# The mask that spreads queries over edges in a graph attention kernel, made by ScalarE instead of VectorE

## The chip, the core and the metric

The kernel runs on one core of a Trainium2 chip. The core has five engines that run side by side and meet only at semaphores: TensorE (PE in the rows) multiplies matrices, VectorE (DVE) and ScalarE (ACT) compute elementwise, GpSimd (POOL) here issues indirect gathers, and SyncE (SP) here watches transfers and loads rows. ACTq, DVEq, POOLq and SPq are the instruction queues (sequencers) of those engines: register work, semaphore waits, loads of registers and DMA issues run there. The metric is the device time of one execution in microseconds (us). The kernel before takes 7133.87 us, the median of 3 runs (7126.53 to 7137.48).

## The reference

Two graph networks run one after the other on 6,250 nodes and 100,000 edges, each with a residual and a layer norm around it. The first is four graph convolutions, which this change does not touch. The second is two attention layers:

```python
xn = _layernorm(x, ln1_g[l], ln1_b[l])
...
q = (xp @ Wq[l] + bq[l]).reshape(n, H, HD)          # k, v likewise
att = jnp.einsum('ehd,ehd->eh', q[dst], k[src]) / scale
att = jnp.nan_to_num(jnp.clip(att, -50.0, 50.0), nan=0.0, posinf=50.0, neginf=-50.0)
m = jax.ops.segment_max(att, dst, num_segments=n)
ex = jnp.exp(att - m[dst])
s = jax.ops.segment_sum(ex, dst, num_segments=n)
alpha = ex / (s[dst] + 1e-16)
msg = (v[src] * alpha[:, :, None]).reshape(-1, D)
aggr = jax.ops.segment_sum(msg, dst, num_segments=n)
x = x + (aggr @ Wo[l] + bo[l])
h = jax.nn.gelu(_layernorm(x, ln2_g[l], ln2_b[l]) @ W1[l] + b1[l], approximate=False)
x = x + (h @ W2[l] + b2[l])
```

Here D = 128, H = 8 heads and HD = 16; `dst` is sorted and falls with a square law on the low node numbers, so the first tiles of nodes have many edges and the last ones few.

## The kernel before, in words

Nodes lie in 49 tiles of 128 (the partitions). Edges are sorted by destination and lie in 196 groups of 4 x 128 = 512 edges, an edge on a partition. A tile's edges are a range of groups `first..last`; the last group of a tile is the first of the next one, since a group can hold edges of both. Six passes run one after the other: p = 0 to 3 are convolutions, p = 4 and 5 the attention layers ("first" and "second" attention pass here). In an attention pass a step of the loop handles one pair of tiles (even, then odd), and beside its edges the node work of earlier pairs in a pipeline: norms, feed-forward product with Gelu, and in the first pass also queries, keys and values of the next layer.

For a group `g` of tile `t` the engines do this:

- GpSimd issues 4 indirect gathers (L1391) of the key and value rows into a ring of 7 groups. It may refill a slot when `groups_freed` says that ScalarE has seen the group's message.
- SyncE loads the group's destination numbers as a row on all partitions, `dst_row` (a ring of 4), waits for the gathers of group `g`, and then says `group_landed` for `g` and `dst_ready` for `g + 1`.
- The node mask `mask_t[node, edge] = (dst_row[edge] == node_id[node])` is 128x512. VectorE makes it (L796). In the profile its tile is called `conv_only`, of which it is a part. It has two slots: slot 0 for the group's own tile and slot 1 for the next tile, used at the last group of a tile, which belongs to both.
- TensorE spreads the queries over the edges: `spread_q` (L1777) multiplies the mask with the tile's query rows, 4 times (8 times at a group of two tiles), and writes `q_ps`. It waits for `mask_t_ready`.
- VectorE multiplies queries with keys (L990), sums per head (L993), clips (L997, L998) and adds (L1001, `logits`). Then it makes the other mask, `masks[edge, node]` for the sums (L808), which waits until TensorE has added the group before.
- ScalarE takes the exp (L1502), VectorE multiplies it with the values into the message (L1005), and TensorE adds it into the tile's sums (`add_group`, L1787). In between TensorE runs 5 filler products (L1758).

The order is written out by hand in `attend_step` of each engine. `weigh` is the VectorE part of a group and stands in front with the mask of group `g + 1` (`ahead`), so a mask is made one group early. `close` ends a tile: the mask of the next tile at the shared last group, some node work, and the mask of the sums. ScalarE's part of a group is only the exp and the word `groups_freed`; between groups it does the node work: column copies with scale and bias (L1518, L1616), the Gelu of a pair (L1629) with a table load before it and one behind it (L1633, with a dummy exp `warm`), the copies of queries, keys and values (L1540, L1541) and the stores. At each step every engine loads the group ranges of its two tiles into registers (L459).

## Time and profile before

| | |
|---|---|
| median of the timed runs | 7133.87 us |
| the profiled execution's own time | 7115.46 us |
| its span | 7112.9 us |
| TensorE busy | 4951.4 us (70%) |
| VectorE busy | 3873.3 us (54%), 10619 instructions |
| ScalarE busy | 678.4 us (10%), 1598 instructions |
| GpSimd busy | 3368.2 us (47%) |
| attention passes | from about 4090 us to the end |

Busy time is the time in which an engine computes; waits, register work and DMA issues are not in it. No engine is busy all the time, so shares do not say what bounds the kernel: for that one reads, stretch by stretch, which wait ends last. In a row of the timeline the bracket is the engine's idle time before the instruction and what ended it. Rows of one line that follow each other are merged (x8, for instance, for the four f32 products of a group).

### The profile page before, as it was taken

How to read it: one execution, taken by the hardware profiler on the slowest of the kernel's cores; microseconds unless marked ns; L12 is line 12 of the kernel's file. 1: busy time of each engine (PE TensorE's matmuls, PEld its weight loads, DVE VectorE, ACT ScalarE, POOL GpSimd, SP SyncE). 2: the span in 40 equal slices, each digit the busy share in tenths (PEclk: the TensorE clock that was granted, in tenths of full speed). 3: DMA queues.
4: the chain of work that ended last, by engine and by line, in shares of the span. 5: the costliest groups of instructions: out<-in, count | busy, mean ns of one | idle time of the engine just before them, and what ended most of it. 6: DMA issues, size and time to landing. Idle time of an engine off the chain costs nothing.

```text
span 7112.9 us, 114495 instructions
## 1 busy us (share of the span) xinstructions
PE 4951.4 (70%) x25317; PEld 3761.7 (53%) x25540; DVE 3873.3 (54%) x10619; ACT 678.4 (10%) x1598; POOL 3368.2 (47%) x3512
## 2 busy tenths in 40 slices
PE   2677656767778778887477666677777666666666
PEld 1121345555666656676455544566666444555555
DVE  8644346663344423444345556677667556666665
ACT  0011100000000000000001100011112100111111
POOL 0000265664555465553666566666443366665441
PEclk9975667668989989999688788899889788888887
DMA  1011323223333333343233244444333244443331
GB/s 47 18 54 72 116 74 91 83 81 104 116 116 120 105 115 112 110 128 104 61 116 98 77 120 120 123 121 121 104 100 87 80 121 118 123 120 104 92 90 49
DMA packets 308014, 695.45 MB, mean 98 GB/s; under 512 B 68843, under 2 KB 118116, under 8 KB 306526
## 3 DMA queue, kind: packets, MB, share of 16 engines
q0 software_dynamic: 146944, 381.90, 19.1%
q10 hardware_dynamic: 94612, 196.31, 8.2%
q1 hardware_dynamic: 66250, 114.82, 5.4%
q8 instruction: 88, 1.44, 0.1%
q14 instruction: 120, 0.98, 0.0%
HBM read 624.93 MB, written 67.83 MB: 97 GB/s over the span
## 4 chain that ended last, share of the span: by engine, by line
PE 32%; DVE 18%; issue 16%; DMA 14%; POOL 10%; DVEq 7%; ACT 2%; POOLq 0%; SPq 0%; ACTq 0%
DMA ring<-rows,idx_stage 12%; POOL ring L1391 10%; PE acc_ps L1853 7%; PE acc_ps L1835 7%; PE q_ps L1777 4%; PE acc_ps L1787 3%; PE bank L1889 2%; DVE wide L990 1%; DVE dots L993 1%; DVE even_rows L582 1%; DVE masks L808 1%; PE bank L2028 1%; PE acc_ps L1747 1%; DVEq L459 1%; DVEq L466 1%
## 5 line engine op out<-in xcount | busy, mean ns | idle before, releaser
L1391 POOL DMA_INDIRECT ring<-rows,idx_stage x3360 | 3329.0, 991 | 2482.3 <-DMA ring<-rows,idx_stage 914.5
L1853 PE MATMUL acc_ps<-ring,masks 128*128 x4800 | 1147.8, 400 | 681.9 <-SPq L1304 352.2
L1853 PEld LDWEIGHTS acc_ps<-ring,masks 128*128 128x128 f32 x4800 | 921.4, 241 | 879.7 <-issue 802.8
L1777 PE MATMUL q_ps<-odd_rows,conv_only 128*128 (+1 forms) x3904 | 733.5, 354 | 710.9 <-DVE conv_only L796 708.4
L788 DVE SCALAR_TENSOR_TENSOR masks<-dst_f,neg_first,lane 128x256 f32<-128x256 f32 x1200 | 546.1, 483 | 1057.7 <-PE acc_ps L1853 891.6
L1777 PEld LDWEIGHTS q_ps<-odd_rows,conv_only 128*128 128x128 f32 x3904 | 648.6, 255 | 782.0 <-issue 778.2
L1787 PE MATMUL acc_ps<-msg,masks 128*128 x3904 | 625.5, 309 | 191.2 <-DVE msg L1005 191.1
L1787 PEld LDWEIGHTS acc_ps<-msg,masks 128*128 128x128 f32 x3904 | 571.8, 216 | 318.3 <-issue 309.9
L1376 POOL COPY idx_stage<-src_idx 128x28 int32 (+1 forms) x126 | 33.1, 262 | 1157.0 <-DVE bias_part L727 809.5
L808 DVE SCALAR_TENSOR_TENSOR masks<-dst_f,neg_first,lane 128x512 f32<-128x512 f32 x488 | 366.6, 751 | 238.7 <-PE acc_ps L1787 231.0
L796 DVE TENSOR_SCALAR conv_only<-conv_only,node_id 128x512 f32 x488 | 243.6, 499 | 438.0 <-SPq L1333 267.3
L1758 PE MATMUL q_ps<-bias_rows,zeros_bf 128*128 128x512 bf16 x1228 | 370.6, 430 | 22.3 <-issue 13.9
L710 DVE TENSOR_SCALAR ring<-ring 128x784 f16 x434 | 184.0, 424 | 316.6 <-PE q_ps L1748 117.8
L1005 DVE TENSOR_TENSOR msg<-ring,msg x392 | 270.8, 691 | 72.0 <-ACT msg L1502 70.9
L889 DVE TENSOR_SCALAR rows<-acc_ps,dinv 128x256 f32<-128x256 f32 (+1 forms) x147 | 64.0, 435 | 398.0 <-PE q_ps L1762 333.2
L993 DVE TENSOR_REDUCE dots<-wide 128x32 f32<-128x512 f32 x392 | 269.0, 686 | 13.4
L990 DVE TENSOR_TENSOR wide<-q_ps,ring 128x512 f32 x392 | 270.2, 689 | 7.3 <-PE q_ps L1777 2.0
L582 DVE TENSOR_TENSOR even_rows<-lane_bf,even_rows 128x1024 bf16<-128x1024 bf16 x196 | 238.6, 1217 | 52.9 <-PE bank L1713 43.1
L1502 ACT ACTIVATE msg<-logits 128x32 f32 x392 | 89.1, 227 | 1681.5 <-DVE logits L1001 1681.5
L1758 PEld LDWEIGHTS q_ps<-bias_rows,zeros_bf 128*128 128x128 bf16 x1450 | 160.1, 110 | 142.0 <-issue 57.7
L1713 PE MATMUL bank<-even_rows 128*128 128x49 bf16 x1568 | 90.9, 210 | 186.5 <-DVE even_rows L584 186.5
L1661 ACT ACTIVATE wide<-q_ps 128x512 f32<-128x512 f32 (+2 forms) x75 | 38.9, 519 | 1899.7 <-PE q_ps L1762 1899.7
(278 smaller groups left out, 6202.0 us busy)
## 6 DMA issues: line engine op xcount, KB each, us to landing
conv_only<-dst_rows SPq DMA_DIRECT2D x394, 256.0 KB, 3.3
ring<-rows,idx_stage POOLq DMA_INDIRECT x3360, 2.8
adjacency<-odd_rows ACTq DMA_DIRECT2D x10, 3136.0 KB, 8.8
conv_only<-adjacency ACTq DMA_DIRECT2D x70, 384.0 KB, 4.4
msg<-adjacency ACTq DMA_DIRECT2D x60, 384.0 KB
wide<-adjacency ACTq DMA_DIRECT2D x60, 384.0 KB, 4.4
turn_b<-adjacency ACTq DMA_DIRECT2D x60, 384.0 KB, 4.2
part<-adjacency ACTq DMA_DIRECT2D x30, 448.0 KB, 3.7
```

Source lines behind the costliest of these rows:

```text
L582: vec.tensor_tensor(one_lo[:, j0:j1, :], lane_bf[:, :].unsqueeze(1).broadcast_to([P, k, P]), lo_f[:, e, bass.ds(b * HC + j0, k)].unsqueeze ...
L788: return vec.scalar_tensor_tensor(out=to, in0=dst_f[:, bass.ds(col + 2 * h, 2)].unsqueeze(2).broadcast_to([P, 2, P]), scalar=neg_first[:, ...
L808: vec.scalar_tensor_tensor(out=masks[:, u, :, :], in0=dst_f[:, bass.ds(col, GC)].unsqueeze(2).broadcast_to([P, GC, P]), scalar=neg_first[: ...
L990: vec.tensor_tensor(qk[:, :, :], q_ps[:, k, :].rearrange("p a (c f) -> p (a c) f", f=D), ring[:, bass.ds(slot, GC), 0:D], ALU.mult).then_i ...
L993: vec.tensor_reduce(dots[:, :, :], qk[:, :, :].rearrange("p c (h d) -> p c h d", h=H), AX_X, ALU.add).then_inc(edge_step, 1)
L1005: vec.tensor_tensor(msg[:, k, :, 0:D].rearrange("p a c (h d) -> p (a c) h d", h=H), ring[:, bass.ds(slot, GC), D:KV].rearrange("p c (h d) ...
L1391: pool.indirect_dma_start(ring[:, j, 0:WIDTH[p]], None, tables[p][:, :], bass.IndirectOffsetOnAxis(ap=idx_stage[:, half, j:j + 1], axis=0) ...
L1758: pe.matmul(bank, zeros_bf[:, :], bias_rows[:, 0:512], start=True, stop=True)
L1777: ins = pe.matmul(to, mask_t[:, u, j, :], q_rows[:, bass.ds(t + u, 1), :].rearrange("p a f -> p (a f)"), start=u == 0, stop=u == nxt)
L1787: ins = pe.matmul(acc(t, 0, MSG), masks[:, u, j, :], msg[:, bass.ds(g & 1, 1), j, :].rearrange("p a m -> p (a m)"), start=False, stop=fina ...
L1835: ins = pe.matmul(to, parts(p)[q % PART_RING][:, r * P:(r + 1) * P], rows_in[p][:, k, 0:WIDTH[p]], start=False, stop=k == TILES - 1)
L1853: ins = pe.matmul(to, masks[:, u, j, :], rhs, start=False, stop=final and j == GC - 1)
```

## The change

ScalarE makes the node mask with two activations in place: `near = |dst_row - node|` with the negated node number as bias per partition (`neg_node`, made once by GpSimd), and `relu(1 - near)`, which is 1 where both numbers are equal and 0 elsewhere. Between the two it waits for its own first one (`mask_t_near`). VectorE's `spread_mask` and its calls are gone. On ScalarE the mask of group `g + 1` stands in front of the exp of group `g` in `weigh`, behind a wait for `q_ready`; the mask of the next tile at the shared last group stands at the end of `weigh_rest`. TensorE's and SyncE's code are the same.

```diff
-            def spread_mask(p, t, g, u):
-
-                vec.wait_ge(dst_ready, (p - CONVS) * (GROUPS * sweeps + 1) + g + 1)
-                vec.tensor_scalar(mask_t[:, u, :, :].rearrange("p c n -> p (c n)"),
-                                  dst_row[:, bass.ds(dst_slot(p, sweeps, laps, g), 1), :].rearrange("p a n -> p (a n)"),
-                                  node_id[:, bass.ds(t, 1)], None, ALU.is_equal).then_inc(mask_t_ready, 1)
...
-            def weigh(p, t, g, back, ahead, u):
+            def weigh(p, t, g, back, u):
                 slot = (g % RG) * GC
                 k = bass.ds(g & 1, 1)
                 vec.wait_ge(q_ready, group_at(p, sweeps, g))
-                if ahead:
-                    spread_mask(p, t, g + 1, 0)
...
                     else:
-                        spread_mask(p, t + 1, at[1], 1)
                         node_work()
...
+            pool.iota(neg_node[:, :], [[-P, TILES]], base=0, channel_multiplier=-1, **exact)
...
-            def weigh(p, g):
-
+            def spread_mask(p, t, g, u):
+
+                act.wait_ge(dst_ready, (p - CONVS) * (GROUPS * sweeps + 1) + g + 1)
+                act.sem_inc(banks_seen, 1)
+                spread = mask_t[:, u, :, :].rearrange("p c n -> p (c n)")
+                act.activation(spread, dst_row[:, bass.ds(dst_slot(p, sweeps, laps, g), 1), :].rearrange("p a n -> p (a n)"),
+                               ACT.Abs, bias=neg_node[:, bass.ds(t, 1)]).then_inc(mask_t_near, 1)
+                act.wait_ge(mask_t_near, visit(p - CONVS, sweeps, t, g) + 1)
+                act.activation(spread, spread, ACT.Relu, scale=-1.0, bias=1.0).then_inc(mask_t_ready, 1)
+
+            def weigh(p, t, g, ahead):
+
+                if ahead:
+                    act.wait_ge(q_ready, group_at(p, sweeps, g))
+                    spread_mask(p, t, g + 1, 0)
                 act.wait_ge(logits_ready, group_at(p, sweeps, g))
...
-            def weigh_rest(p, at):
+            def weigh_rest(p, t, at):
...
-                        weigh(p, g)
+                        weigh(p, t, g, True)
                 with act.Else():
                     pass
+                if isinstance(t, int) and t == TILES - 1:
+                    weigh(p, t, last, False)
+                else:
+                    act.wait_ge(q_ready, group_at(p, sweeps, last - 1))
+                    spread_mask(p, t + 1, last, 1)
```

Where the instructions now stand, at the places that matter most. First ScalarE in the odd tile of a pair of the first attention pass, right behind Gelu, its second table load and the `warm` exp. Before, the next group's exp (L1502) followed:

```order
L1511 COMPARE_AND_BRANCH
L1512 UNCONDITIONAL_BRANCH
L1512 ISA
L1502 REGISTER_ALU
L1502 ISA
L1502 ACTIVATE msg<-logits 128x4x8
```

Now (the exp is L1506, and L1495 and L1498 are the two halves of the mask):

```order
L1515 COMPARE_AND_BRANCH
L1516 UNCONDITIONAL_BRANCH
L1516 ISA
L1492 REGISTER_ALU
L1495 REGISTER_ALU x2
L1495 ISA
L1495 ACTIVATE conv_only<-conv_only,neg_node 128x512
L1497 ISA
L1498 ACTIVATE conv_only<-conv_only 128x512
L1506 REGISTER_ALU
L1506 ISA
L1506 ACTIVATE msg<-logits 128x4x8
```

Both halves of the mask moved in between the branch and the exp. Second, ScalarE at the end of a step of the first attention pass, from the store of keys and values to the first exp of the next pair. Before:

```order
L1544 DMA rows<-wide 128x2x256
L130 REGISTER_ALU
L130 COMPARE_AND_BRANCH
L459 TENSOR_LOAD ranges
L1501 REGISTER_ALU
L1502 REGISTER_ALU
L1502 ISA
L1502 ACTIVATE msg<-logits 128x4x8
```

Now:

```order
L1553 DMA rows<-wide 128x2x256
L130 REGISTER_ALU
L130 COMPARE_AND_BRANCH
L460 TENSOR_LOAD ranges
L1503 REGISTER_ALU
L1492 REGISTER_ALU
L1495 REGISTER_ALU x2
L1495 ISA
L1495 ACTIVATE conv_only<-conv_only,neg_node 128x512
L1497 REGISTER_ALU
L1498 ACTIVATE conv_only<-conv_only 128x512
L1506 REGISTER_ALU
```

The mask, for which TensorE waits, now stands behind the DMA issue and the load of the ranges on ScalarE. Third, VectorE at the same place, from the mask of the sums that closes the odd tile to the product of the next group. Before:

```order
L808 SCALAR_TENSOR_TENSOR masks<-dst_f,neg_first,lane 128x512
L1234 ISA
L130 REGISTER_ALU
L130 COMPARE_AND_BRANCH
L459 TENSOR_LOAD ranges
L986 REGISTER_ALU
L795 REGISTER_ALU
L796 REGISTER_ALU x2
L796 ISA
L796 TENSOR_SCALAR conv_only<-conv_only,node_id 128x512
L989 ISA
L990 REGISTER_ALU
```

Now (the product is L982):

```order
L802 SCALAR_TENSOR_TENSOR masks<-dst_f,neg_first,lane 128x512
L1223 ISA
L130 UNCONDITIONAL_BRANCH
L130 ISA
L460 TENSOR_LOAD ranges
L980 REGISTER_ALU
L981 ISA
L982 REGISTER_ALU
L982 ISA x2
L982 TENSOR_TENSOR wide<-q_ps,ring 128x512
```

The mask and its register rows are gone between the load and the product.

## Rows read from the trace of the kernel before

**Rows 1.** The page's group: xcount | busy us, mean ns | idle before it.

```profile
L796 DVE TENSOR_SCALAR conv_only<-conv_only,node_id 128x512 f32 x488 | 243.6, 499 | 438.0 <-SPq L1333 267.3
```

**Rows 2.** Windows: us, busy (x instructions) of PE, PEld, DVE, ACT, POOL; clock, DMA, GB/s.

```profile
4100.00:4592.00 492.00, 314.53 (x1665) 240.81 (x1717) 298.35 (x664) 23.58 (x86) 299.39 (x312) 0.84 0.41 121
4592.00:5504.00 912.00, 680.20 (x3972) 553.38 (x4029) 642.81 (x1767) 173.92 (x433) 474.59 (x493) 0.89 0.37 108
5600.00:6096.00 496.00, 315.58 (x1669) 238.88 (x1720) 298.11 (x664) 23.70 (x87) 304.38 (x315) 0.84 0.42 120
6096.00:7035.00 939.00, 646.21 (x3697) 549.23 (x3755) 610.12 (x1653) 132.22 (x297) 469.06 (x492) 0.83 0.35 102
```

**Rows 3.** Waits in 4100:4592: waiter <- releaser: total us, times, longest.

```profile
DVE conv_only L796 <- SPq L1333: 125.0, 53, 4.1
```

**Rows 4.** Waits in 4592:5504, the late part of the first attention pass.

```profile
PE q_ps L1777 <- DVE conv_only L796: 172.3, 79, 3.8
...
POOL ring L1391 <- ACTq L1506: 143.8, 41, 9.4
...
DVE conv_only L796 <- SPq L1333: 3.0, 4, 1.7
```

**Rows 5.** ScalarE's range loads, 4592:5504 and 6096:7035: ns min/median/max, starts.

```profile
L459 ACTq TENSOR_LOAD <-ranges x20: 1741/2184/2403, 4610.3 to 5485.2; - x20
...
L459 ACTq TENSOR_LOAD <-ranges x20: 1714/1724/1750, 6114.5 to 7003.3; - x20
```

**Rows 6.** Chain of waits in 5000:5510, shares by line.

```profile
by line: issue 14.1%; PE acc_ps L1787 13.4%; PE q_ps L1777 12.6%; DVE wide L990 4.9%; DVE dots L993 4.9%; DVE masks L808 4.5%; PE bank L2028 4.4%; DVEq L459 3.3%; ACT L1633 3.3%; DVE conv_only L796 3.2%; DVE msg L1005 3.0%; DVEq L796 2.3%; 
```

**Rows 7.** ScalarE's groups by form.

```profile
L1672 ACT ACTIVATE wide<-rows 128x512 f32<-128x512 f32 x72 | 45.3, 629 | 442.7 <-DVE rows L962 442.7
...
L1616 ACT ACTIVATE turn_b<-bank 128x256 f32<-128x256 f32 x48 | 18.4, 383 | 274.6 <-PE bank L1762 186.8 <-PE bank L1934 87.9
```

**Rows 8.** Timeline, odd tile, first pass: start, duration, row [idle <- releaser].

```profile
5465.20 1.15 PE L1777 MATMUL q_ps<-odd_rows,conv_only 128*128 x8 [0.37 <-DVE conv_only L796]
5465.20 0.47 ACT L1518 ACTIVATE turn_b<-bank,b_pd 128x256 f32<-128x256 f32 x1
...
5468.49 1.19 PE L1787 MATMUL acc_ps<-msg,masks 128*128 x8 [1.05 <-DVE msg L1005]
...
5474.86 0.21 ACT L1502 ACTIVATE msg<-logits 128x32 f32 x1
5475.35 0.69 DVE L1005 TENSOR_TENSOR msg<-ring,msg  x1 [1.48 <-ACT msg L1502]
5476.13 0.49 DVE L796 TENSOR_SCALAR conv_only<-conv_only,node_id 128x512 f32 x1
...
5476.95 3.65 PE L1777 MATMUL q_ps<-odd_rows,conv_only 128*128 x16 [3.44 <-DVE conv_only L796]
...
5482.50 0.75 DVE L808 SCALAR_TENSOR_TENSOR masks<-dst_f,neg_first,lane 128x512 f32<-128x512 f32 x1
```

**Rows 9.** Timeline, the even tile behind it.

```profile
5484.43 0.39 ACTq L1544 DMA_DIRECT2D rows<-wide  x1
...
5485.67 1.15 PE L1777 MATMUL q_ps<-odd_rows,conv_only 128*128 x8 [2.13 <-DVE conv_only L796]
...
5489.09 1.19 PE L1787 MATMUL acc_ps<-msg,masks 128*128 x8 [1.19 <-DVE msg L1005]
...
5492.45 1.02 ACT L1518 ACTIVATE turn_b<-bank,cols 128x256 f32<-128x256 f32 x2 [4.59 <-PE bank L1762]
...
5493.93 0.23 ACT L1502 ACTIVATE msg<-logits 128x32 f32 x1 [0.46 <-DVE logits L1001]
...
5496.02 2.05 PE L1777 MATMUL q_ps<-odd_rows,conv_only 128*128 x16 [1.40 <-DVE conv_only L796]
```

**Rows 10.** Timeline of a pair in the second pass.

```profile
6676.99 3.78 PE L1777 MATMUL q_ps<-odd_rows,conv_only 128*128 x16 [3.95 <-DVE conv_only L796]
...
6686.56 2.07 PE L1777 MATMUL q_ps<-odd_rows,conv_only 128*128 x8 [4.30 <-DVE conv_only L796]
```

27 lines of the change are left out of this document (12 added, 15 removed).

## The prediction

> **What bounds the kernel now.** The change touches only the two attention passes, some 3,000 us of a 7,112.9 us span, so I read in this order: the page's group of the mask instruction, the windows of the two passes, the waits in them, the shares of the chain, and last two tile pairs instruction by instruction. The page shows 488 masks on VectorE at 499 ns each, 243.6 us in all [rows 1]. TensorE waits for this very line.
>
> The windows split each pass in two. While tiles have many groups of edges, GpSimd issues 312 gathers (78 groups of four) in 492 us, one group per 6.3 us, and ScalarE does almost nothing; later, at 4592:5504 and 6096:7035, 493 and 492 gathers take 912 and 939 us, 7.4 and 7.6 us per group [rows 2]. The waits say who sets the pace. In the early stretch VectorE waits 125.0 us for SyncE's word that a group and its row are there [rows 3]: gathers set the pace and computing has slack. In the late one that wait is down to 3.0 us, GpSimd waits 143.8 us for ScalarE to free groups, and TensorE waits 172.3 us in 79 places for VectorE's mask [rows 4]. So late in each pass a serial chain over TensorE, VectorE and ScalarE binds, and in it TensorE already stands waiting for masks: a mask that comes later costs there at once. That chain has 20 tile pairs in each pass, one load of the group ranges each [rows 5], so 45.6 us per pair in the first and 47.0 in the second.
>
> **The removed part.** VectorE loses 488 instructions of about 0.49 us in front of the product of queries and keys. On the chain this line has 3.2% of 5000:5510, and its register work 2.3% [rows 6]. The saving is real only where VectorE comes last; where TensorE waits for the mask, what counts is when ScalarE has it.
>
> **The added part.** No row shows this Abs or this Relu, but the same Relu on 128x512 f32 in SBUF takes 629 ns [rows 7]. A bias read per partition adds 0.09 us: an activation of 128x256 takes 383 ns without and 470 ns with it [rows 7, 8]. Two of them and a small gap give 1.26 us at least, 1.53 at most (both with bias, 0.1 between); I take 1.37. The mask itself thus takes 0.88 us longer. The order adds register work: VectorE did that under its message, but ScalarE waits for the end of the message, so it comes behind. I take 0.45 us from the message's end to Abs: the 0.28 us between ScalarE's exp and VectorE's message [rows 8] and the register rows in front of Abs; its bounds are 0.1 (all hidden) and 0.9. From a mask's end to TensorE's start is 0.33 us (5476.62 to 5476.95) [rows 8], which stays.
>
> The Trainium skill (ScalarE: Activation LUTs, Rules for kernel authors) says to use VectorE for relu and simple arithmetic. For this size the rows agree: 0.49 against 0.63 us, and two of the latter are wanted.
>
> The larger cost is ScalarE's place in the order. Its queue is in order: a mask stands in front of the exp of its own group and behind Gelu, both table loads, the column copies and, at the end of a pair, the query copies, a DMA issue and the load of the ranges. I walk through one pair of the first pass, as a shift against before.
>
> First the odd tile [rows 8]. ScalarE's bias copy ends at 5465.67, so the mask is there at 5467.05 and TensorE spreads queries at 5467.4 instead of 5465.20. Its sums waited for the message until 5468.49; now spreading and filler bring them to 5469.6, +1.1. The feed-forward product and Gelu move with them. Behind Gelu the exp at 5474.86 gets a mask ahead of it: +1.1 +1.37, so the message is +2.5 late. The mask for two tiles was made right after the message; now 0.45 + 1.37 + 0.33 us pass from the message's end (5476.04 + 2.5) to TensorE: 5480.7 instead of 5476.95, +3.75. VectorE's mask of the sums at 5482.50 waited for nobody, so 1.0 us hides there: +2.8.
>
> Then the even tile [rows 9]. TensorE's +3.75 reaches the copies: the DMA issue moves from 5484.43 to 5488.2. Only then come ScalarE's range load (the last one of rows 5 starts 0.77 us behind that issue and lasts 2.18 us), Abs and Relu: TensorE spreads at 5492.9 instead of 5485.67. Its 2.13 us wait becomes some 6. The sums follow 2.3 us later: 5495.2 instead of 5489.09, +6.1. The column copies end at 5493.47 + 6.1, then mask and exp: exp +7.1. The two-tile mask is +8.4 at 5496.02, and so is the next pair. **One pair costs +8.4 us, 20 pairs +168.**
>
> The second pass has no query copies and no second column copy. In a pair there [rows 10] I get, by the same steps, +2.5 at the two-tile mask (6676.99), and then a gain: ScalarE is idle at the step's end, so its mask is ready before VectorE has loaded its ranges, and TensorE's 4.30 us wait at 6686.56 goes. The shift falls to +0.8, since the sums then wait for the message. Behind the column copy and the output's DMA issue it grows again by mask (+1.37) and the slower two-tile mask: +2.6 per pair, 20 pairs +52.
>
> Gains to set against it: the late stretches hold 985 gathers, 246 groups, or 86 beyond the four weighings per pair that I walked. Inside such a run VectorE comes last and each saves 0.49 us, 42 us in all; I take 20, as the row load of the next group has to keep up. TensorE's longer stand at the pair's end also matters: spreading took 1.15 us behind a 2.13 us wait [rows 9] and 2.07 us behind one of 4.30 [rows 10]; at 0.92 us in half of the first pass's pairs that is +9. In the gather-paced stretches 125.0 us of slack cover the change; I take 0.
>
> **Sum:** 168 + 52 - 20 + 9 = +209 us on the profiled execution's own 7,115.5 us, 7,324. That execution lies 18 us below the timed median of 7,133.9, so the forecast is 7,133.9 + 209, about 7,340. Bounds: some six masks and two register waits of a pair's walk lie on the path (four and two in the second pass); with 1.26 us per mask and 0.1 us of register work that is 20 x (6 + 4) x 0.11 + 40 x 2 x 0.35, some -50; with 1.53 and 0.9 us some +70; if half of ScalarE's queueing is hidden by waits that I took for fixed, -90; if TensorE's clock falls in more places, +40. Its own range is 7,230 to 7,440.
>
> **Rivals.**
> *ScalarE's masks are early* (slower, little). If ScalarE reaches masks ahead of its other work more often than I read, only the two-tile masks are late, 1.33 us twice per pair: 80 x 1.33 = 106, less about 40 of saved VectorE time, so 7,200. Against it: the order rows put the mask behind Gelu and the range load.
>
> *VectorE is the bound* (faster). If the mask always comes before TensorE is done with its sums, the chain loses what the line has in it: 3.2% + 2.3% [rows 6] of the 1,851 late us, 102 us, so 7,030. It decides where TensorE has nothing to wait for at a mask. Against it: 172.3 us of exactly that wait [rows 4].
>
> *Hidden* (same). If gathers set the pace throughout, nothing moves: 7,134. For it: rows 3; against it: GpSimd's 143.8 us wait for ScalarE [rows 4].
>
> *Gathers get faster* (faster). If VectorE's mask holds up GpSimd while it issues, its removal shortens the gather-paced stretches: at most 0.49 us for each of 157 groups [rows 2], 77 us, so 7,057, if nothing else grows. Against it: GpSimd's busy time per gather is 0.96 us in the early and the late stretch alike, 299.39/312 and 474.59/493 [rows 2]. The Trainium skill (SBUF — State Buffer, Who interferes with whom) states that a VectorE tensor_scalar in a two-port mode and GpSimd block each other. These rows don't settle it.
>
> **Chances.** Forecast 0.80; masks early 0.07; VectorE the bound 0.06; hidden 0.04; gathers faster 0.03. A measurement of this kernel tells about 0.2% (14 us) from no change: faster 0.09, same 0.04, slower 0.87. The range of 7,190 to 7,430 leaves out the faster and hidden cases and a little at the top.
>
> **What would show it.** In the changed profile ScalarE is busy some 1,330 us (678 + 488 x 1.34) and VectorE some 3,630. The Abs and Relu lines stand at 0.63 to 0.72 us. TensorE's wait for the mask, now from ScalarE, grows in 4592:5504's pairs from 172.3 us to well over 300. A late pair takes 8 us more in the first pass and 2 to 3 in the second; stretches before 4592 and 5600:6096 keep their length. VectorE's message waits for exp after Gelu more than the 1.48 us of rows 8. It would be wrong if those pairs keep their length, if a table load stands between Abs and Exp, or if gathers in the early stretches come closer together.

## The result, and the profile after

The changed kernel takes 7,529.12 us (median of 4 runs, 7,519.48 to 7,538.38), the kernel before 7,133.61 in the same comparison: a ratio of 1.0555, 95% interval 1.0537 to 1.0574. The forecast was 7,340 (7,190 to 7,430): the direction is right, and the cost of 395 us is nearly twice the 209 that were forecast.

The profiled execution took 7,529.56 us. In the page of its profile (the summary of one traced execution), ScalarE's two halves of the mask and TensorE's wait for them answer to [rows 1] (xcount | busy us, mean ns | idle before it):

```profile
L1783 PE MATMUL q_ps<-odd_rows,conv_only 128*128 (+1 forms) x3904 | 770.0, 366 | 1071.0 <-ACT conv_only L1498 1068.4
...
L1495 ACT ACTIVATE conv_only<-conv_only,neg_node 128x512 f32 x488 | 351.4, 720 | 1009.8 <-SPq L1322 390.6
...
L1498 ACT ACTIVATE conv_only<-conv_only 128x512 f32<-128x512 f32 x488 | 307.2, 629 | 15.4
```

A mask takes 0.720 + 0.629 us on ScalarE where VectorE took 0.499, as forecast. TensorE's spreading waits 1,068 us for it in all.

The windows, as in [rows 2]: 492 us of the early part of each pass, and then the late parts. Those begin and end at the first table load of Gelu in a pair, so that a window after holds the same 20 pairs as 4592.18:5503.91 (911.7 us) and 6096.06:7035.01 (939.0 us) before.

```profile
4112.00:4604.00 492.00, 322.84 (x1708) 247.89 (x1709) 257.94 (x582) 132.62 (x248) 300.78 (x312) 0.82 0.42 120
5861.00:6353.00 492.00, 317.02 (x1716) 247.97 (x1716) 255.65 (x581) 132.51 (x248) 302.03 (x314) 0.83 0.42 121
...
4604.15:5753.48 1149.33, 747.92 (x4020) 616.27 (x4019) 569.86 (x1609) 371.96 (x746) 461.58 (x492) 0.79 0.30 85
6353.17:7449.43 1096.26, 728.28 (x3752) 604.45 (x3751) 538.99 (x1496) 339.79 (x611) 462.13 (x492) 0.76 0.30 87
```

The early parts issue as many gathers per us as before (312 and 314 in 492 us): there the change costs next to nothing, and VectorE's wait for SyncE's word is about what it was (134.3 us against 125.0 in [rows 3]). The waits in 4112:4604:

```profile
DVE wide L982 <- SPq L1320: 134.3, 46, 4.4
```

The late ones grow by 237.6 and 157.3 us, 395 of the 415 us by which the span grew. The other 20 us lie ahead of the two late parts (12.0 and 7.5 us); the runs of this kernel differ by as much. Per pair that is +11.9 and +7.9 us; forecast were +8.4 and +2.6. So of the 186 us that the forecast lacks, 70 lie in the first pass's walk and 105 in the second's; the other 11 are the sum's -20 and +9. The granted clock falls from 0.89 to 0.79 and from 0.83 to 0.76, and TensorE is busy longer with the same work: its weight loads alone, which are nearly all recorded, from 553.38 and 549.23 us [rows 2] to 616.27 and 604.45. ScalarE is busy 1,317.7 us and VectorE 3,646.4 in the page (forecast some 1,330 and 3,630), and no table load was added.

The waits in 4604:5753, to compare with [rows 4] (us in total, times, longest), and the shares of the chain in 5200:5750, to compare with [rows 6]:

```profile
PE q_ps L1783 <- ACT conv_only L1498: 398.0, 108, 6.3
POOL ring L1381 <- ACTq L1510: 370.0, 59, 12.4
DVE masks L802 <- PE acc_ps L1793: 170.9, 50, 7.2
...
DVE msg L997 <- ACT msg L1506: 126.6, 64, 4.3
```

```profile
by line: PE q_ps L1783 21.6%; PE acc_ps L1793 13.6%; issue 12.8%; ACT conv_only L1495 8.2%; PE q_ps L1764 6.8%; ACT conv_only L1498 5.8%; ACTq L460 4.2%; PE bank L1948 3.1%; PE bank L1768 2.8%; DVE msg L997 2.7%; ACT L1641 2.3%; PE bank L20
```

The wait for the mask grew from 172.3 us to 398.0. The filler (L1764, `keep_busy`) is in none of the shares that [rows 6] prints, the smallest of them 2.3%; now it has 6.8% of the chain. Spreading itself went from 12.6 to 21.6%.

The timeline of the pair that answers to [rows 8] and [rows 9] (start, duration, row [idle <- releaser]):

```profile
5703.16 0.47 ACT L1527 ACTIVATE turn_b<-bank,b_pd 128x256 f32<-128x256 f32 x1
5703.57 0.72 ACT L1495 ACTIVATE conv_only<-conv_only,neg_node 128x512 f32 x1
...
5705.29 1.15 PE L1783 MATMUL q_ps<-odd_rows,conv_only 128*128 x8 [2.50 <-ACT conv_only L1498]
...
5707.36 1.09 PE L1793 MATMUL acc_ps<-msg,masks 128*128 x8
...
5714.91 0.21 ACT L1506 ACTIVATE msg<-logits 128x32 f32 x1
5715.40 0.69 DVE L997 TENSOR_TENSOR msg<-ring,msg  x1 [3.13 <-ACT msg L1506]
...
5716.77 0.72 ACT L1495 ACTIVATE conv_only<-conv_only,neg_node 128x512 f32 x1 [1.65 <-DVE msg L997]
...
5718.48 3.46 PE L1783 MATMUL q_ps<-odd_rows,conv_only 128*128 x16 [6.19 <-ACT conv_only L1498]
...
5723.06 0.75 DVE L802 SCALAR_TENSOR_TENSOR masks<-dst_f,neg_first,lane 128x512 f32<-128x512 f32 x1 [1.26 <-PE acc_ps L1793]
...
5725.77 0.40 ACTq L1553 DMA_DIRECT2D rows<-wide  x1
...
5731.04 2.07 PE L1783 MATMUL q_ps<-odd_rows,conv_only 128*128 x8 [6.16 <-ACT conv_only L1498]
5732.90 2.34 PE L1764 MATMUL q_ps<-bias_rows,zeros_bf 128*128 128x512 bf16 x5
5735.03 1.14 PE L1793 MATMUL acc_ps<-msg,masks 128*128 x8
...
5740.55 0.21 ACT L1506 ACTIVATE msg<-logits 128x32 f32 x1
...
5744.10 2.66 PE L1783 MATMUL q_ps<-odd_rows,conv_only 128*128 x16 [3.59 <-ACT conv_only L1498]
5746.56 2.02 PE L1793 MATMUL acc_ps<-msg,masks 128*128 x8
```

Counted from the end of ScalarE's bias copy (5465.67 before, 5703.63 after, 237.96 apart), each row of the table gives its shift:

| step | before | after - 237.96 | shift | forecast |
|---|---|---|---|---|
| odd tile: spreading | 5465.20 | 5467.33 | +2.1 | +2.2 |
| sums | 5468.49 | 5469.40 | +0.9 | +1.1 |
| exp behind Gelu | 5474.86 | 5476.95 | +2.1 | +2.5 |
| spreading for two tiles | 5476.95 | 5480.52 | +3.6 | +3.75 |
| mask of the sums | 5482.50 | 5485.10 | +2.6 | +2.8 |
| even tile: spreading | 5485.67 | 5493.08 | +7.4 | +7.2 |
| sums | 5489.09 | 5497.07 | **+8.0** | +6.1 |
| exp | 5493.93 | 5502.59 | +8.7 | +7.1 |
| spreading for two tiles | 5496.02 | 5506.14 | **+10.1** | +8.4 |
| next pair's table load | 5503.91 | 5515.52 | **+11.6** | +8.4 |

Down to the even tile's spreading the walk holds within 0.4 us. Then it parts: behind a wait of 6.16 us that spreading takes 2.07 us instead of 1.15 [rows 9], and the filler 2.34 us for its five matmuls, where most sets of four or five take 1.03 to 1.24 at the higher level. At the lower level both stand between the mask and the sums. At the end of the tile it happens again, 2.66 for 2.05 us in spreading and 2.02 for 1.09 in the sums.

That pair is no exception. In the late part of the first pass 3 of 77 recorded sets of filler ran at 0.4 us or more per matmul before, and 29 of 75 after; in the second pass 16 of 77 and 45 of 76. Spreading, filler and sums together keep TensorE busy some 73 us longer in the late part of the first pass and some 68 in that of the second, for the same matmuls (busy time in the late windows of L1777, L1758 and L1787 before and L1783, L1764 and L1793 after; the filler scaled to equal counts, as some records are missing): 3.6 and 3.4 us per pair, of which waits may hide a part.

In the second pass it begins earlier. These are rows of the pair of [rows 10] before that [rows 10] leaves out, and then the same pair after:

```profile
6659.65 0.38 ACT L1616 ACTIVATE turn_b<-bank 128x256 f32<-128x256 f32 x1 [6.91 <-PE bank L1762]
...
6669.11 1.16 PE L1777 MATMUL q_ps<-odd_rows,conv_only 128*128 x8
...
6690.56 1.83 PE L1787 MATMUL acc_ps<-msg,masks 128*128 x8
```

```profile
7009.03 0.38 ACT L1624 ACTIVATE turn_b<-bank 128x256 f32<-128x256 f32 x1 [6.28 <-PE bank L1768]
...
7011.28 1.71 PE L1783 MATMUL q_ps<-odd_rows,conv_only 128*128 x8 [2.29 <-ACT conv_only L1498]
...
7023.02 2.07 PE L1783 MATMUL q_ps<-odd_rows,conv_only 128*128 x8 [3.08 <-ACT conv_only L1498]
...
7024.89 2.34 PE L1764 MATMUL q_ps<-bias_rows,zeros_bf 128*128 128x512 bf16 x5
...
7029.90 0.75 DVE L997 TENSOR_TENSOR msg<-ring,msg  x1
...
7031.44 0.72 ACT L1495 ACTIVATE conv_only<-conv_only,neg_node 128x512 f32 x1 [3.37 <-DVE msg L997]
...
7033.15 3.77 PE L1783 MATMUL q_ps<-odd_rows,conv_only 128*128 x16 [4.18 <-ACT conv_only L1498]
...
7039.26 1.15 PE L1783 MATMUL q_ps<-odd_rows,conv_only 128*128 x8 [0.52 <-ACT conv_only L1498]
...
7043.00 2.31 PE L1764 MATMUL q_ps<-bias_rows,zeros_bf 128*128 128x512 bf16 x5 [2.58 <-DVE wide L982]
...
7045.78 2.18 PE L1793 MATMUL acc_ps<-msg,masks 128*128 x8 [0.47 <-DVE msg L997]
```

Counted from the column copies (6659.65 and 7009.03, 349.38 us apart), the spreading at 6669.11 is 4.5 us late: this odd tile has one more group than the tile above, and that group's mask now stands behind Gelu and the second table load, so TensorE waits 3.08 us where it had no wait. Spreading, filler and sums behind it then run at the lower level. At the two-tile mask (6676.99 before) the shift is +6.8 us, where +2.5 was forecast.

TensorE's 4.30 us wait at the step's boundary did go, as forecast (0.52 at 7039.26). Nothing was gained by it: VectorE's load of the ranges stands behind its mask of the sums, which waits for TensorE's sums, so the product, the filler behind it and the sums stay late; the sums by 5.8 us (6690.56 and 7045.78).

### The profile page after: what moved, and what is told of

It reads as the page before. It is cut to its first block, busy times and chain, and to the rows that moved or that the text cites. A ratio compares the mean times of both kernels' runs of the same rounds, so it can differ in the third digit from the quotient of the medians.

```text
span 7527.8 us, 116246 instructions
## 1 busy us (share of the span) xinstructions
PE 5112.8 (68%) x25539; PEld 3903.1 (52%) x25540; DVE 3646.4 (48%) x10131; ACT 1317.7 (18%) x2574; POOL 3354.5 (45%) x3513
## 4 chain that ended last, share of the span: by engine, by line
PE 36%; issue 16%; DVE 13%; DMA 13%; POOL 9%; ACT 6%; DVEq 5%; ACTq 2%; POOLq 0%; SPq 0%
DMA ring<-rows,idx_stage 11%; POOL ring L1381 9%; PE q_ps L1783 7%; PE acc_ps L1841 6%; PE acc_ps L1859 6%; PE acc_ps L1793 5%; ACT conv_only L1495 2%; PE q_ps L1764 2%; ACT conv_only L1498 2%; PE bank L1895 2%; DVE even_rows L583 1%; DVE msg L997 1%; DVEq L711 1%; PE bank L1768 1%; DVE wide L982 1%
## 5 line engine op out<-in xcount | busy, mean ns | idle before, releaser
L1783 PE MATMUL q_ps<-odd_rows,conv_only 128*128 (+1 forms) x3904 | 770.0, 366 | 1071.0 <-ACT conv_only L1498 1068.4
L1783 PEld LDWEIGHTS q_ps<-odd_rows,conv_only 128*128 128x128 f32 x3904 | 679.8, 266 | 1147.4 <-issue 1147.3
L1793 PEld LDWEIGHTS acc_ps<-msg,masks 128*128 128x128 f32 x3904 | 662.0, 241 | 126.6 <-issue 103.8
L1793 PE MATMUL acc_ps<-msg,masks 128*128 x3904 | 683.5, 330 | 35.0 <-DVE msg L997 34.9
L1764 PE MATMUL q_ps<-bias_rows,zeros_bf 128*128 128x512 bf16 x1450 | 494.5, 487 | 61.8 <-DVE wide L982 61.8
L1495 ACT ACTIVATE conv_only<-conv_only,neg_node 128x512 f32 x488 | 351.4, 720 | 1009.8 <-SPq L1322 390.6
L982 DVE TENSOR_TENSOR wide<-q_ps,ring 128x512 f32 x392 | 270.8, 691 | 517.7 <-SPq L1320 278.4
L1498 ACT ACTIVATE conv_only<-conv_only 128x512 f32<-128x512 f32 x488 | 307.2, 629 | 15.4
L1764 PEld LDWEIGHTS q_ps<-bias_rows,zeros_bf 128*128 128x128 bf16 x1450 | 171.2, 120 | 239.1 <-issue 173.9
```

The costliest lines, as they stand in the source:

```text
L982: vec.tensor_tensor(qk[:, :, :], q_ps[:, k, :].rearrange("p a (c f) -> p (a c) f", f=D), ring[:, bass.ds(slot, GC), 0:D], ALU.mult).then_i ...
L1495: act.activation(spread, dst_row[:, bass.ds(dst_slot(p, sweeps, laps, g), 1), :].rearrange("p a n -> p (a n)"), ACT.Abs, bias=neg_node[:, ...
L1498: act.activation(spread, spread, ACT.Relu, scale=-1.0, bias=1.0).then_inc(mask_t_ready, 1)
L1764: pe.matmul(bank, zeros_bf[:, :], bias_rows[:, 0:512], start=True, stop=True)
L1783: ins = pe.matmul(to, mask_t[:, u, j, :], q_rows[:, bass.ds(t + u, 1), :].rearrange("p a f -> p (a f)"), start=u == 0, stop=u == nxt)
L1793: ins = pe.matmul(acc(t, 0, MSG), masks[:, u, j, :], msg[:, bass.ds(g & 1, 1), j, :].rearrange("p a m -> p (a m)"), start=False, stop=fina ...
```

## The experiments

Theories after the result. *C, the clock*: what the walk missed is TensorE at the lower of its two levels behind longer waits, filler included. *Q, the queue*: what it did foresee comes from the mask's place in ScalarE's queue and less from its length. *L*: the length alone. The runs were made in five comparisons, each on a chip of its own with the kernel before beside it. The kernel before took 7,139 us in the first (the first four kernels below), 7,134 in the third (the changed kernel again, the moved wait again, masks two ahead and the next first mask), but 7,418 in the second, 7,324 in the fourth and 7,345 in the fifth. So each ratio is taken to the kernel before on the same chip, and times are set against each other only within a comparison or where the chips are alike. "Late parts" are the 20 pairs of each pass as above.

**No filler**, in the changed kernel and in the one before: `-EDGE_FILL = 5`, `+EDGE_FILL = 0`.

> The changed kernel with no filler matmuls in the attention passes (none instead of five per group). Theory A: in the changed kernel the filler and TensorE's lower clock are part of the serial chain. In the late stretches 380 and some 270 fillers of 484 to 530 ns were recorded, in sets of up to 2.3 us, between spreading and the sums; taken out they give back 100 to 300 us, so 7,230 to 7,430 us. Variant A2: the filler still pays for itself in clock, so that spreading and sums grow when it goes and the time stays within 40 us of 7,529. Theory B (only ScalarE's queue and the mask's own length count): the filler lies under VectorE's work as before, 7,510 to 7,550, and pairs in the late first pass keep 57.5 us.

> The kernel before with no filler matmuls in the attention passes. The partner of the changed kernel without filler. Theory A: the filler lies under VectorE's work here, so its loss saves little; the clock may fall in the records: 7,100 to 7,190 us, and the distance between the two kernels without filler shrinks from 395 us to 150 to 300. Theory B: the distance stays 395 us to within 30, whatever this kernel does.

The changed kernel gained: 7,470.09, ratio 1.0469 (1.0451 to 1.0486), less than the 100 us or more that I expected. The one before lost: 7,255.00, 1.0161 (1.0144 to 1.0178), more than I expected. Their distance shrank to 215 us, as theory A says. Windows of the late parts, the changed kernel first:

```profile
4606.60:5721.66 1115.06, 683.95 (x3640) 610.18 (x3639) 572.36 (x1609) 371.86 (x746) 463.01 (x492) 0.77 0.31 88
6316.90:7388.32 1071.42, 621.71 (x3370) 573.38 (x3368) 539.10 (x1496) 339.93 (x612) 463.34 (x492) 0.77 0.31 89
```

```profile
4608.17:5584.18 976.01, 666.98 (x3644) 587.36 (x3642) 641.22 (x1765) 171.85 (x433) 467.67 (x492) 0.79 0.35 101
6174.52:7170.89 996.37, 629.63 (x3370) 576.42 (x3368) 610.99 (x1651) 132.31 (x298) 464.85 (x491) 0.74 0.33 96
```

So the filler buys the kernel before 116 us, with a clock of 0.89 and 0.83 instead of 0.79 and 0.74. In the changed kernel it no longer buys a clock (0.79 and 0.76 with, 0.77 and 0.77 without) and costs 59. Without filler on either side the change costs 215 us: 7.0 us per pair in the first pass (1,115.1 - 976.0 over 20) and 3.8 in the second. The walk had 8.4 and 2.6. Its total, 209 us, agrees with 215, but it is too high in one pass and too low in the other by about the same, so the agreement is partly luck. The other 180 us come only with the filler in place: what it gave the kernel before and takes from the changed one. Clock level and filler on the path are not told apart by these two kernels.

**Only one of the two operations:**

```diff
-                act.wait_ge(mask_t_near, visit(p - CONVS, sweeps, t, g) + 1)
-                act.activation(spread, spread, ACT.Relu, scale=-1.0, bias=1.0).then_inc(mask_t_ready, 1)
```

> The changed kernel without the second operation of the mask (the Relu), so the mask that TensorE uses is the absolute difference, and the attention is of other numbers; everything else is as in the changed kernel. It halves the mask's length on ScalarE, by 0.66 us, and leaves its place in ScalarE's queue. If all of a pair's six masks of the first pass and four of the second are on the path, 40 pairs give 20 x 10 x 0.66 = 132 us back, so some 7,400 us; theory A (TensorE's clock goes down with long waits) adds to it: 7,330 to 7,380. Theory B', the place in the queue and not the length costs the time: 7,450 to 7,500.

7,330.80, 1.0268 (1.0251 to 1.0285): 198 us come back for 0.66 us per mask, where ten masks (six in a pair of the first pass, four in one of the second) times 20 give 132 at face value. The clock comes up to 0.81 in both passes. The theory with the clock holds (7,330 to 7,380). The length counts, by half as much again as its own time. TensorE spreads other numbers here (the mask is wrong without Relu), but the instructions and their sizes are the same.

**The two-tile mask earlier, on VectorE**, in the kernel before:

```diff
                 sum_mask(p, t, g, back, u)
+                if last is not None:
+                    with vec.If(last < g + 2):
+                        spread_mask(p, t + 1, g + 1, 1)
+                    with vec.Else():
+                        pass
                 vec.wait_ge(exp_ready, group_at(p, sweeps, g))
...
-                        spread_mask(p, t + 1, at[1], 1)
                         node_work()
```

> The kernel before, but VectorE makes the mask for two tiles in the last round of a tile's loop, ahead of its wait for exp, and not behind the message. It tests how much of before's time already hangs on where one mask stands. Theory: TensorE waits 3.6 to 4.3 us for this mask at one place per tile pair and less at others; 40 pairs give back 1 to 3 us each, 7,010 to 7,090. Rival: the wait only moves to the sums, which need the message anyway, and the register work of the new branch costs 0.1 to 0.3 us per group: 7,120 to 7,180.

7,057.66, 0.9883 (0.9866 to 0.9899), 81 us faster: 883.0 and 905.7 us in the late parts, 1.4 and 1.7 us per pair. Before's own order was not the best one: one mask in front of a wait, not behind it, is worth a fifth of what the change costs.

**ScalarE frees a group behind the next mask**, in the changed kernel:

```diff
                     spread_mask(p, t, g + 1, 0)
+                if not (isinstance(t, int) and t == 0 and first):
+                    act.wait_ge(msg_ready, group_at(p, sweeps, g) - 1)
+                    act.sem_inc(groups_freed, 1)
                 act.wait_ge(logits_ready, group_at(p, sweeps, g))
...
-                act.wait_ge(msg_ready, group_at(p, sweeps, g))
-                act.sem_inc(groups_freed, 1)
+                if not ahead:
+                    act.wait_ge(msg_ready, group_at(p, sweeps, g))
+                    act.sem_inc(groups_freed, 1)
```

> The changed kernel with ScalarE's wait for a group's message (and the word that frees the group) moved behind the next group's mask: ScalarE then makes the mask of group g+1 while VectorE still works at message g-1, as TensorE spreads group g ahead of the sums of g-1. Length, operations and count of the masks stay. Theory Q (the order of ScalarE's queue costs the time, not the 1.35 us of the mask): the masks leave the path, TensorE's wait for them falls from 1,068 us to under 500, TensorE's clock in the late stretches comes back from 0.79 and 0.76 towards 0.89 and 0.83, and since VectorE no longer has the mask, the time comes out below the kernel before: 6,980 to 7,130 us. Theory L (the length costs it): most of the wait stays, 7,350 to 7,500. Rival: groups are freed later by up to one group and the row loads and gathers fall behind, 7,200 to 7,350, with VectorE's wait for SyncE up.

On the slower chip 1.0228 (1.0196 to 1.0259), and later beside the changed kernel:

> The changed kernel itself, unaltered, beside the others, since the kernel before took 7,418 us on the chip of the last four comparisons and 7,134 to 7,139 on the chip of the first: it shows whether the cost of the change, 395 us or a ratio of 1.055, is the same where the whole program is slower. Expected 1.050 to 1.060 in ratio to the kernel before if the cost is a count of instructions and waits; more than 1.065 if it grows with what makes that chip slow.

> The changed kernel with the wait for the message moved behind the next group's mask, a second time, since its 1.023 in ratio to the kernel before came without the changed kernel beside it. If the ratio holds, this one reordering gives back 3.2 of the 5.5 per cent: 1.018 to 1.028 here. If its ratio depends on the chip: 1.03 to 1.045.

The changed kernel repeats: 7,527.49, 1.0555. With the wait moved 7,341.62, 1.0293 (1.0276 to 1.0310). Operations and their number are the same, and 186 us, nearly half of the cost, are back (windows of its late parts):

```profile
4603.66:5640.68 1037.02, 697.21 (x4016) 567.25 (x4014) 567.33 (x1607) 374.54 (x747) 466.25 (x493) 0.85 0.33 95
6239.25:7247.67 1008.42, 683.14 (x3745) 570.62 (x3744) 533.16 (x1495) 340.11 (x611) 465.80 (x491) 0.81 0.33 95
```

I had expected it to beat the kernel before, with TensorE's wait for masks under 500 us; the page has 935, after 1,068. The timeline (of the first of the two runs) shows why not: the first mask of an even tile still stands behind ScalarE's DMA issue and load of the ranges, and TensorE waits 6.6 us for it.

```profile
5240.23 0.40 ACTq L1556 DMA_DIRECT2D rows<-wide  x1
...
5243.68 0.72 ACT L1495 ACTIVATE conv_only<-conv_only,neg_node 128x512 f32 x1 [3.63 <-issue]
...
5245.51 2.07 PE L1786 MATMUL q_ps<-odd_rows,conv_only 128*128 x8 [6.59 <-ACT conv_only L1498]
```

**Masks two ahead**, all of them by ScalarE, at the first moment at which their place is free:

```diff
+            def masks_ahead(p, t, g, last):
+                with act.If(g + 1 < last):
+                    act.wait_ge(q_ready, group_at(p, sweeps, g + 1))
+                    spread_mask(p, t, g + 2, 0)
+                with act.Else():
+                    if not (isinstance(t, int) and t == TILES - 1):
+                        spread_mask(p, t + 1, g + 1, 1)
+                        act.wait_ge(q_ready, group_at(p, sweeps, g + 1))
+                        spread_mask(p, t + 1, g + 2, 0)
```

It is called behind each exp, ahead of the wait for the message.

> The changed kernel with ScalarE making each mask as early as its place is free: behind the exp of group g it waits for TensorE to have spread g+1 and makes the mask of g+2 (at a tile's end the one for two tiles, and then the next tile's first), all ahead of its wait for message g, its column copies, Gelu and the load of the ranges. The same two operations per mask. Theory Q (the place in ScalarE's queue, not the operations): TensorE's wait for the mask falls under 250 us, clock back, VectorE relieved of the mask: ratio 0.965 to 0.99, faster than the kernel before. Rival 1: ScalarE now stands at TensorE's spreading and its exps and copies come late: 0.99 to 1.02. Rival 2 (length counts): 1.03 and more.

7,087.23, 0.9930 (0.9914 to 0.9947), in the range of rival 1. The same 976 activations cost 395 us in the one order, and in the other the kernel is 0.7% faster than the kernel before, whose own masks stand later than they could. The late parts and, in the page, the wait (idle before it in the last column):

```profile
4606.52:5521.37 914.85, 695.24 (x4033) 568.96 (x4032) 569.97 (x1610) 380.73 (x746) 469.73 (x493) 0.88 0.37 108
6107.07:7015.51 908.44, 652.48 (x3759) 541.69 (x3758) 535.14 (x1496) 341.89 (x612) 472.32 (x492) 0.85 0.37 106
...
L1791 PE MATMUL q_ps<-odd_rows,conv_only 128*128 (+1 forms) x3904 | 671.9, 332 | 592.6 <-ACT conv_only L1498 588.3
...
L1495 ACT ACTIVATE conv_only<-conv_only,neg_node 128x512 f32 x488 | 351.9, 721 | 962.0 <-PE q_ps L1791 454.3
```

TensorE still waits 588 us for masks, not under 250: ScalarE itself waits 454 us for TensorE's spreading of the group before. But the clock is back (0.88 and 0.85). The fair partner of this kernel is VectorE with early masks too, and that is the next one.

**VectorE's next first mask early as well** (on top of the early two-tile mask): in `close`, `+vec.wait_ge(q_ready, group_at(p, sweeps, at[1]))` and `+spread_mask(p, t + 1, at[1] + 1, 0)` behind the node work.

> The kernel before with VectorE's two-tile mask ahead of its wait for exp (0.988 in ratio by itself) and the first mask of the next tile made at the end of the tile, ahead of VectorE's load of the ranges and not behind it. TensorE's wait at the start of the even tile was 2.1 us in the first and 4.3 us in the second pass: 20 x 2.1 + 20 x 4.3 = 128 us at most, of which the sums' own wait for the message keeps half. Expected 0.976 to 0.984. Rival: the range load was hidden and nothing is gained, 0.986 to 0.992.

7,054.29, 0.9891 (0.9874 to 0.9909): nothing beyond the 0.9883 of the one mask. The rival holds, though not by a hidden load: spreading's wait falls from 703 to 535 us, the waits of sums and filler grow by 102 (176 to 230 and 24 to 71). A wait that moves.

This kernel ran beside the one with ScalarE's masks two ahead, on the same chip: 7,054 us with VectorE's early masks, 7,087 with ScalarE's, and the slowest run of the one (7,070.51) is faster than the fastest of the other (7,077.62). So with the masks early on either engine ScalarE's is still some 30 us or 0.4% slower, though VectorE is rid of 244 us of work. The orders are alike but not equal, so this is no pure price of the engine. So the 0.7% above speaks for the order and not for the move.

**Which masks cost how much.** In the changed kernel VectorE makes either the two-tile mask again (`+spread_mask(p, t + 1, at[1], 1)` in its `close`, and none in ScalarE's `weigh_rest`) or the first mask of each tile (`+if u == 1: spread_mask(p, t, g + 1, 0)` in its `weigh`). The third (last of the three texts) makes each mask twice on VectorE in the kernel before, with a wait between.

> The changed kernel with the masks for two tiles (48 in each pass) made by VectorE again, behind the message as in the kernel before; ScalarE makes all the others. By the steps of the prediction the two-tile mask costs 1.25 us more than its message's delay at each of two places per pair in either pass: 80 x 1.3 = 104 us, and what TensorE's clock adds to that: 7,529 - 104 = 7,425, with the clock 7,330 to 7,400. If the cost of the change lies mostly in these masks: under 7,300. If it lies in ScalarE's masks behind Gelu and the range load: 7,420 to 7,500.

> The changed kernel with the first mask of every tile (the one that ScalarE makes behind its column copies, Gelu, table loads or the load of the group ranges) made by VectorE again, as in the kernel before; ScalarE makes the masks inside a tile and those for two tiles. By the steps of the prediction this mask costs 2.2 us at the odd tile of the first pass, some 2.3 at the even one, and gains in the second pass at the step's boundary: 20 x 4.5 = 90 in the first pass, 0 in the second: 7,440. With the clock's part 7,350 to 7,440. If first masks hardly matter: 7,480 to 7,530. If they are the main cost: under 7,300.

> The kernel before with every mask made twice by VectorE, the second time behind a wait for the first, into the same place: the mask comes 0.5 to 0.65 us later, and VectorE works 244 us more; nothing goes to ScalarE. It prices lateness alone, without ScalarE's queue. Theory: in the late stretches (246 groups) every group's mask is on VectorE's chain, 246 x 0.55 = 135 us, and TensorE's clock falls a little with the longer waits: 7,270 to 7,350. Rival (the price of lateness is small, ScalarE's queue makes the 395 us): 7,180 to 7,240. If lateness and clock alone explain the change: 7,400 and more.

On the slowest chip: 1.0278 (1.0227 to 1.0329), 1.0386 (1.0354 to 1.0417) and 1.0200 (1.0164 to 1.0237). The first two are where the sums of the steps with the clock's part put them, the third at the low end of its theory. The first two again, on a chip where before takes 7,324:

> The changed kernel with the masks for two tiles made by VectorE again, a second time, since it ran on the slower chip (1.028 in ratio). By the prediction's steps (80 masks in the late stretches, 1.3 us each) 1.040; the first run says that they cost half of all: 1.026 to 1.032.

> The changed kernel with the first mask of each tile made by VectorE again, a second time, since it ran on the slower chip (1.039 in ratio). By the prediction's steps 90 us in the first pass and nothing in the second, 1.043; from the first run 1.036 to 1.043. In the second pass's late pairs little should come back (under 40 us of 157), in the first 70 us or more of 238.

1.0273 (1.0242 to 1.0304) and 1.0304 (1.0267 to 1.0342). Against the changed kernel on another chip of nearly the same speed (1.0498, below) the two-tile masks hold 165 us by the ratios (92 and 93 us less in the late parts), and the first masks 142 (74 and 41 in the late parts). The two runs of the first-mask kernel lie further apart than both intervals, and below what I expected of the second, so its share is rough; 41 us in the second pass, where I had 0, I can't split further. Twice the mask on VectorE, some 0.5 us later and in no queue of ScalarE's, costs 169 us. That is lateness and VectorE's 244 us of added work together; this kernel doesn't tell them apart. The change makes a mask 0.88 us longer. With the kernel without Relu this says that the length is a good part of the result as the order stands, and masks two ahead show that most of it can be hidden. The parts overlap: 180 us with the filler, 186 with the moved wait, 198 with Relu, 165 and 142 with the two kinds of mask add up to far more than 395, since each of them shortens the same waits.

**The filler inside the wait.** The changed kernel with its filler ahead of spreading, while the mask isn't there:

```diff
-    EDGE_FILL = 5
+    EDGE_FILL = 0
...
+                pe.wait_ge(q_used, group_at(p, sweeps, g))
+                keep_busy(q_ps[:, bass.ds(g & 1, 1), :].rearrange("p a f -> p (a f)"), 5)
                 pe.wait_ge(mask_t_ready, visit(p - CONVS, sweeps, t + nxt, g) + 1)
-                pe.wait_ge(q_used, group_at(p, sweeps, g))
```

This is more filler than before, though I meant it to be equal: the old place had none at a tile's last group, the new one has five ahead of each spreading. The page counts 1,960 filler matmuls after the edit and 1,450 in the changed kernel.

> The changed kernel with the five filler matmuls of a group moved: not between spreading and the sums, but ahead of spreading, while TensorE would wait for the mask. As much filler as before, in the wait. Theory C (a part of the 395 us is TensorE's own work at the lower clock level after long waits for the mask): the wait is filled, the granted clock in the late stretches comes up from 0.79 and 0.76 to 0.83 or more, TensorE's busy time of equal work falls, and the kernel is faster than with no filler at all (7,470 us): 7,380 to 7,450. Rival 1: the clock has little to do with it and the filler is only in the way or not: 7,460 to 7,490 (no filler) where it hides, or 7,520 to 7,560 where the filler makes spreading late. Rival 2: the clock comes up but the filler's own 1.0 to 2.3 us stands in the way at short waits: 7,450 to 7,500 with a clock above 0.83.

> The changed kernel with its filler ahead of spreading, a second time, now with the changed kernel beside it on the same chip. From the first run (ratio 1.032, granted clock 0.82 and 0.84 in the late stretches): 1.028 to 1.038, and 1.5 to 2.5 per cent faster than the changed kernel beside it. If the first run's gain came from its chip: within 1 per cent of the changed kernel without filler, 1.042 to 1.050.

> The changed kernel itself on the same chip as the one with the filler in the wait: 1.050 to 1.058 in ratio to the kernel before where the chip is like the first ones, 1.045 to 1.055 where it is one of the slower ones.

1.0324 (1.0284 to 1.0364) and, on the next chip, 7,565.62, 1.0307 (1.0279 to 1.0334), where the changed kernel takes 7,705.33, 1.0498 (1.0471 to 1.0524). 140 us come back by filler in another place, and a third more of it, with the masks as late as ever. Late parts of the changed kernel on that chip, then with the filler in the wait:

```profile
4666.37:5859.22 1192.85, 750.11 (x4024) 618.76 (x4023) 570.13 (x1609) 371.77 (x746) 444.79 (x476) 0.79 0.28 80
6489.16:7623.46 1134.30, 729.68 (x3750) 605.44 (x3749) 538.37 (x1495) 338.69 (x611) 443.24 (x473) 0.74 0.29 82
```

```profile
4674.74:5804.88 1130.14, 796.41 (x4214) 637.90 (x4214) 569.92 (x1604) 371.98 (x747) 455.04 (x485) 0.82 0.30 86
6408.71:7485.02 1076.31, 718.85 (x3955) 591.38 (x3953) 537.70 (x1492) 339.77 (x611) 455.43 (x483) 0.83 0.30 88
```

The clock rises from 0.79 and 0.74 to 0.82 and 0.83, and the late parts are 63 and 58 us shorter. Part of that is the filler no longer standing between spreading and sums; removing it altogether gave 59 us in total, so I estimate some 80 of the 140 for the clock (two comparisons, two chips). That the clock can be had back without a single earlier mask, and that time comes with it, is the clearest sign for theory C.

**The version that beats both**: the early two-tile mask, and five more filler matmuls per tile ahead of its wait (the edit above with `5 if nxt else 0` and `EDGE_FILL` left at 5, on the kernel before with the early mask).

> The kernel before with VectorE's two-tile mask ahead of its wait for exp (0.988 in ratio) and five more filler matmuls per tile, ahead of TensorE's wait for that mask (3 us at one such place of the second pass, followed by spreading that took 3.77 us where it takes 2.05 elsewhere). Theory C: the clock in the second pass's late stretch comes up from 0.85 and the time falls by 20 to 50 us: 0.981 to 0.986. Rival: the added filler stands in the way where the wait is short: 0.988 to 0.995.

7,192.38 where before takes 7,324.42: 0.9810 (0.9783 to 0.9837), the lowest ratio of all, at a clock of 0.90 and 0.87 in the late parts (0.89 and 0.85 without the added filler). That the filler gave the last 0.7 per cent is not shown: it rests on ratios from two chips, 0.9810 against 0.9883, and the ratio of one edit differed by up to 0.8 points between chips.

## Why the prediction was wrong

*What bounds, and where it would cost*: right. The early parts kept their pace, 395 of 415 us lie in the late ones. The waits named grew (172.3 to 398.0 us for the mask).

*The price of a mask, 1.37 us*: right (0.720 + 0.03 + 0.629 = 1.38). *0.45 us from message to Abs*: low. It took 0.68 (5716.09 to 5716.77) in the first pass and 0.79 in the second (message 7029.90 + 0.75 to 7031.44), inside the bounds of 0.1 and 0.9. Some 0.3 us on 80 two-tile masks would be 24 us, an estimate.

*The walk through the first pass's pair*: right to 0.4 us in its first six steps. **The step that failed is "TensorE's longer stand at the pair's end also matters: ... at 0.92 us in half of the first pass's pairs that is +9."** The row for it was in hand [rows 10], but it was applied to one spreading in ten pairs. In the pair above it happened twice, and it holds for everything that runs at the lower level: spreading +0.9, filler +1.1, then +0.6 and +0.9 at the tile's end, 3.5 us, of which 3.2 (11.6 - 8.4) arrived at the next pair. Over the 20 pairs the rows give 3.6 us of added TensorE time per pair, and 3.5 (11.9 - 8.4) were missing. The filler was priced at nothing: in the rows of before it lay under VectorE's work, and once the mask was late it stood on the path. The two kernels without filler give clock and filler together: 180 of the 395 us, against the +9 of the sum and a bound of +40 for a clock that falls in more places.

*The second pass, +2.6 per pair*: wrong three times, and 105 of the missing 186 us are here. First, "by the same steps" left out the group in the middle of the odd tile, whose mask now waits behind Gelu and the table load: +4.5 us at its spreading, and, with TensorE at the lower level behind it, +6.8 at the two-tile mask, where the walk had +2.5. Second, the gain at the step's boundary didn't come: TensorE's wait went, but the product there hangs on VectorE's range load behind its mask of the sums, and the sums are still 5.8 us late where the walk had +0.8. Third, clock and filler, priced at nothing in this pass, make 4.1 of the 7.9 us by the kernels without filler (7.9 - 3.8).

*-20 for VectorE's saved work*: no run shows it on its own. Masks two ahead do not: they are 0.7% faster than before, but early masks on VectorE alone give more (1.1%). The middle groups, from which the 20 us were taken as a gain, are also those whose masks got late.

*The rivals.* Masks early and VectorE the bound fell for the order as it was made. VectorE the bound needs TensorE to wait for no mask, and no run has that: with masks two ahead 588 us of such waits are left, and the 47 us gained there are fewer than the 81 that one earlier mask gives on VectorE. So its price of 102 us stays untested. *Gathers faster*: GpSimd is busy 300.78 us for 312 gathers, 0.96 us each, as before [rows 2], so no lock of 0.49 us per mask was lifted from it. The Trainium skill (SBUF — State Buffer, Who interferes with whom) has a VectorE tensor_scalar in a two-port mode and GpSimd block each other; no run here shows a gain for GpSimd from its removal.

The Trainium skill (Perfetto Trace Analysis, Optimizing Scalar/DVE Operations) says that an operation with a VectorE performance mode is faster there, and that ScalarE may make sense if VectorE is saturated. VectorE was busy 642.8 of 912 us in the late part before [rows 2], 70%, and the move cost 5.5% in one order; with the masks early on both sides it cost some 0.4%. No run here shows a gain from moving this mask, and the order decided its price, not the busy share.

## What to carry to other kernels

When an operation moves to another engine, ask first behind which waits it will stand in that engine's queue: the same two activations were worth +5.5% behind the message and -0.7% ahead of it. Then give the old engine the same better order before you praise the new one: here VectorE with early masks was faster still (-1.1%). Where the rows show TensorE at both of its clock levels, price a longer wait not only by its length but by all that TensorE does behind it at the lower level, filler included, and try filler in the wait rather than behind it. Walk pairs of several sizes: the group that one pair lacks can be where the new wait lands. And a wait that goes is a gain only if nothing else behind it is as late: follow every input of the next step, also a register load.

## What the runs showed of the hardware

- Filler of 128x512 bf16, five in a row, took 1.03 to 1.24 us (four or five recorded) at the higher level and 2.31 to 2.34 at the lower; spreading of 8 took 1.15 and 2.07. Behind waits of 2.50 and 0.52 us spreading ran at 1.15, behind 2.29 at 1.71, behind 3.08 and 6.16 at 2.07, in these two pairs.
- The same filler was worth 116 us in the kernel before, whose waits are short, and cost 59 in the changed one with its longer waits.
- The same kernel took 7,134 to 7,139, 7,324, 7,345 and 7,418 us on different chips; why is open. The cost of the change was 5.55% on the fast ones and 4.98% on one of the slow ones. Ratios of one edit differed between chips by up to 0.8 points (1.0386 and 1.0304).
